# Two tiles of neighbour sums moved from TensorE matmuls to adding row gathers on GpSimd, passes 3 to 7

## The chip, the cores and the metric

One core of a Trainium2 chip runs the whole program in one launch. The metric is the device time of a launch in microseconds (us); lower is better. Times inside a launch come from one profiled execution.

## The reference, cut to what matters

Two point-cloud layers follow each other. Each of the two batches has 1024 points with 1024 coordinates (`ctx`) and 512 channels (`x`).

```
# layer 0
idx = top_k(-d2(ctx), 8)                   # 8 nearest points, per point
for i in range(4):
    p = leaky_relu(x, 0.01)
    c  = w_center[i] @ p
    gn = w_neighbor[i] @ p[:, idx]         # summed over the 8 neighbours
    x  = (c + gn.sum(neighbours)) / 9 + x
# layer 1
idx = top_k(-d2(ctx), 30)
att = softmax(small network of the neighbours' relative position)
x   = x + sum_k att[k] * x[:, idx[k]]
```

`w_center` and `w_neighbor` are the same input, two 512 x 512 matrices; block 0 uses the first and blocks 1 to 3 the second (an index past the end is clamped). So p and the sum over its neighbours can be added before one product.

## The kernel before, in words

In layer 0 the own point and its 8 neighbours enter with one weight, so the kernel sums the rows of p first and multiplies by the weights after. The sum is a matmul with a 0/1 matrix: `nbr[b]` is 1024 x 1024, has a one where column point takes row point as a neighbour, and a one on the diagonal for the point itself. All of this is done in two parts for accuracy: `p_h` is p rounded to fp32r, `p_l` the rest.

Layer 0 is eight *passes*, `it` = 0 to 7: block `it // 2` of batch `it % 2`. A pass has two stages on TensorE:

- The *aggregation*: 8 units `j` = 0 to 7, each one bank of PSUM. Units 0 to 3 are the four channel tiles of the first 512 points (first half), units 4 to 7 those of the last 512 (second half). A unit is 16 matmuls (8 tiles `m` of source points, `p_h` and `p_l`), in `aggregate` (L1472). ScalarE rounds the result into `q_h` (`q_high`, L718), VectorE writes the rest into `q_l` (`q_low`, L997). Units use banks 0 to 2 in turn, so unit g waits for `q_low` of unit g - 3.
- The *products*, `wp`: 8 tiles `m` of 128 points, 12 matmuls each (L1494 to L1496), in banks 3 to 5 in turn. VectorE adds a tile to `X` in `x_update` (L1003). Product g waits for `x_update` of g - 3.

The p of the next pass is made during the products, in the memory that the old p leaves: ScalarE writes two halves of the leaky ReLU (`p_halves`, L704 and L705), GpSimd joins them (`p_join`, L495), ScalarE rounds (`p_high`, L711), GpSimd subtracts (`p_low`, L500). `p_second`, where the join is, and `p_l` are the same memory, so `p_low` writes over the joined p. The first two units of an aggregation run side by side and wait for `p_low` tile by tile.

Each of the 16 steps of a pass (8 units, 8 products) is a *slot* g = 16 it + s. Every engine's program is written out by hand as a loop over slots, in strict order on each engine. In a slot an engine also does a piece of other work, `side(g)`: selection of neighbours (passes 0 to 2), table lookups of the neighbours' coordinates (slots 45 to 60: passes 2 and 3), the small network with its batch norms, in VectorE and ScalarE steps that wait for each other (passes 4 to 6, `network` and the list `NET`), the index columns (slot 108, pass 6) and the one-hots and spread matmuls of the attention (pass 7, from slot 115). On VectorE `side(g)` stands ahead of `q_low` or `x_update` of the same slot. On ScalarE `p_halves` and `p_high` stand ahead of `side(g)`.

The lookups are fed by broadcasts of index rows from DRAM, 480 KB each, issued by SP into a ring of `NB` = 7 buffers. Behind layer 0 comes `attend`, the attention's own matmuls (L1620 to L1635).

## Time and profile before

| | us |
|---|---|
| three runs | 719.92, 721.95, 722.13 (median 721.95) |
| the profiled execution | 719.64, span 717.9 |
| TensorE busy | 700.1 (98%) |
| VectorE busy | 580.2 (81%) |
| ScalarE busy | 348.1 (48%) |
| GpSimd busy | 250.2 (35%) |
| mean granted TensorE clock | 0.995 of full |

By the starts of the aggregation's and the products' first matmuls in the trace, pass 3 runs from 297.6 to 382.7, pass 4 from 382.7, pass 5 from 433.5, pass 6 from 485.2 and pass 7 from 538.4 to 604.8; the products begin at 348.9, 411.7, 462.5, 515.2 and 575.3. PE is TensorE's matmuls, PEld its weight loads, DVE is VectorE, ACT ScalarE, POOL GpSimd, SP the engine that only issues transfers. A row of a timeline begins with its start and its duration in us, and names in brackets how long the engine was idle before and who released it.

### The profile page before, as it was taken

Reading aid. Unit: us, or ns where it says so; the run is one execution under the profiler, and the core shown is the slowest. Engines: PE = TensorE matmul, PEld = TensorE weight load, DVE = VectorE, ACT = ScalarE, POOL = GpSimd, SP = SyncE. Lnnn points to the kernel's source line nnn. Section 1 sums busy time; section 2 is a strip of 40 time slices with the busy share of each in tenths; the row PEclk is TensorE's granted clock in tenths of the full one; section 3 lists DMA queues with packets and bytes.
Section 4 is the critical chain, followed back from the end, with each engine's and each line's share of the span. In section 5 each row is a group of like instructions: output and inputs, shape, how many; then the busy total and the mean of one; then the engine's idle time right before and its main releaser. Section 6 shows DMA issues by size and latency. Waiting matters only on the chain.

```text
span 717.9 us, 13047 instructions
## 1 busy us (share of the span) xinstructions
PE 700.1 (98%) x5458; PEld 584.5 (81%) x5458; DVE 580.2 (81%) x863; ACT 348.1 (48%) x529; POOL 250.2 (35%) x216
## 2 busy tenths in 40 slices
PE   6999999999999999999999999999998999999998
PEld 4799899778888887888888888877886887888887
DVE  4699999999699899766789798677677799678831
ACT  6456556448417137766892263383472344223210
POOL 2259757646608237400164083064172000000000
PEclk9999999999999999989999999999999999999999
DMA  9510301100000114554400000000000000100101
GB/s 351 178 3 1 117 1 48 41 29 1 1 1 0 62 41 135 190 166 168 167 31 1 1 0 1 0 1 1 0 1 0 2 1 2 42 35 30 46 31 58
DMA packets 21564, 35.66 MB, mean 50 GB/s; under 512 B 10113, under 2 KB 10369, under 8 KB 21505
## 3 DMA queue, kind: packets, MB, share of 16 engines
q1 hardware_dynamic: 20976, 33.78, 14.1%
q10 hardware_dynamic: 528, 1.05, 0.5%
q8 instruction: 43, 0.70, 0.4%
q14 instruction: 17, 0.13, 0.1%
HBM read 30.50 MB, written 4.33 MB: 49 GB/s over the span
## 4 chain that ended last, share of the span: by engine, by line
PE 77%; DVE 12%; POOL 5%; ACT 4%; issue 2%; DMA 1%; SPq 0%; POOLq 0%; ACTq 0%; DVEq 0%
PE bank L1472 25%; PE bank L1494 6%; PE bank L1496 6%; PE bank L1495 6%; PE bank L1519 5%; PE bank L1581 4%; PE bank L1620 4%; PE bank L1622 4%; PE bank L1383 4%; PE bank L1621 4%; PE bank L1385 4%; PE bank L1384 4%; DVE idx L970 2%; DVE vals L968 2%; POOL pts_l L500 1%
## 5 line engine op out<-in xcount | busy, mean ns | idle before, releaser
L1472 PE MATMUL bank<-nbr,pts_h 128*128 128x512 f32 x512 | 203.5, 397 | 4.0 <-DVE pts_l L997 3.9
L1472 PE MATMUL bank<-nbr,pts_l 128*128 128x512 f32 x512 | 200.8, 392 | 0.0
L495 POOL TENSOR_TENSOR p_second<-p_first,p_second 128x512 f32<-128x512 f32 x58 | 77.2, 1335 | 196.1 <-ACT p_second L705 196.1
L1472 PEld LDWEIGHTS bank<-nbr,pts_h 128*128 128x128 f32 x512 | 97.1, 190 | 26.3 <-DVE pts_l L997 4.5
L1472 PEld LDWEIGHTS bank<-nbr,pts_l 128*128 128x128 f32 x512 | 97.0, 190 | 19.9 <-issue 0.2
L718 ACT CAST pts_h<-bank 128x512 fp32r<-128x512 f32 x64 | 37.0, 588 | 155.4 <-PE bank L1472 155.2
L1494 PE MATMUL bank<-wT,pts_h 128*128 128x512 f32 x256 | 101.6, 397 | 0.0
L1496 PE MATMUL bank<-wT,pts_l 128*128 128x512 f32 x256 | 99.8, 390 | 0.0
L1495 PE MATMUL bank<-wT,pts_h 128*128 128x512 f32 x256 | 99.7, 389 | 0.0
L997 DVE TENSOR_TENSOR pts_l<-bank,pts_h 128x512 fp32r<-128x512 f32 x64 | 43.7, 685 | 48.3 <-ACT pts_h L718 47.9
L500 POOL TENSOR_TENSOR pts_l<-p_second,pts_h 128x512 fp32r<-128x512 f32 x58 | 79.1, 1370 | 2.0 <-ACT pts_h L711 2.0
L1383 PE MATMUL bank<-pts_h 128*128 128x512 f32 (+3 forms) x192 | 69.1, 360 | 7.9 <-DVE pts_l L930 7.5
L840 ACT CAST nbr<-bank 128x512 fp32r<-128x512 f32 x64 | 35.2, 590 | 77.9 <-PE bank L1581 77.9
L1384 PE MATMUL bank<-pts_l,pts_h 128*128 128x512 f32 (+3 forms) x192 | 66.4, 346 | 0.0
L1385 PE MATMUL bank<-pts_h,pts_l 128*128 128x512 f32 (+3 forms) x192 | 66.3, 345 | 0.0
L1496 PEld LDWEIGHTS bank<-wT,pts_l 128*128 128x128 f32 x256 | 48.0, 188 | 10.2
L1494 PEld LDWEIGHTS bank<-wT,pts_h 128*128 128x128 f32 x256 | 48.1, 188 | 9.4
L1495 PEld LDWEIGHTS bank<-wT,pts_h 128*128 128x128 f32 x256 | 48.1, 188 | 9.4
L711 ACT CAST pts_h<-p_second 128x512 fp32r<-128x512 f32 x58 | 35.7, 616 | 31.2 <-POOL p_second L495 31.2
L1620 PE MATMUL bank<-pts_h,nbr 128*128 128x512 f32 x120 | 48.7, 406 | 0.6 <-DVE pts_l L1282 0.6
L1003 DVE SCALAR_TENSOR_TENSOR X<-bank,X 128x512 f32<-128x512 f32 x64 | 43.5, 682 | 5.5 <-PE bank L1496 4.8
L1383 PEld LDWEIGHTS bank<-pts_h 128*128 128x128 f32 x192 | 36.8, 191 | 13.0 <-issue 7.2
(212 smaller groups left out, 1341.0 us busy)
## 6 DMA issues: line engine op xcount, KB each, us to landing
more<-a_rows SPq DMA_DIRECT2D x17, 480.0 KB, 4.7
scratch<-a_rows SPq DMA_DIRECT2D x15, 480.0 KB, 4.7
X<-in_ctx SPq DMA_DIRECT2D x12, 512.0 KB, 6.0
out_dram<-X SPq DMA_DIRECT2D x15, 256.0 KB, 2.0
more<-in_ctx SPq DMA_DIRECT2D x4, 512.0 KB, 5.5
X<-in_x SPq DMA_DIRECT2D x2, 1024.0 KB, 5.9
X<-in_x SPq DMA_DIRECT2D x1, 1536.0 KB, 6.8
w_raw<-in_fside_BxSxS SPq DMA_DIRECT2D x1, 1024.0 KB, 11.4
```

The lines of the kernel that those rows point to most:

```text
L495: pool.tensor_tensor(p, a, b, ALU.subtract).then_inc(s_p32, 1)
L500: pool.tensor_tensor(p_l[:, m, :], parts(n)[2], p_h[:, m, :].bitcast(F32), ALU.subtract).then_inc(s_p1, 1)
L997: dve.tensor_tensor(q_l[:, j, :], bank[g % 3][:], q_h[:, j, :].bitcast(F32), ALU.subtract).then_inc(s_ql, 1)
L1003: dve.scalar_tensor_tensor(dst, bank[3 + g % 3][:], 1.0 / (K0 + 1.0), dst, ALU.mult, ALU.add).then_inc(s_xu, 1)
L1383: pe.matmul(o, pts_h[:, k, rows], pts_h[:, k, cols], start=(k == 0), stop=False)
L1384: pe.matmul(o, pts_h[:, k, rows], pts_l[:, k, cols], start=False, stop=False)
L1385: return pe.matmul(o, pts_l[:, k, rows], pts_h[:, k, cols], start=False, stop=(k == KT - 1))
L1472: mm = pe.matmul(bank[u % 3][:], p[:, m, t * P:(t + 1) * P], nbr[b][:, m, hf * HALF:(hf + 1) * HALF], start=(m == 0 and part_ == 0), stop= ...
L1494: pe.matmul(bank[3 + g % 3][:], q_h[:, q, cols], wT[:, hi, t, :], start=(t == 0), stop=False)
L1495: pe.matmul(bank[3 + g % 3][:], q_h[:, q, cols], wT[:, 1 - hi, t, :], start=False, stop=False)
L1496: mm = pe.matmul(bank[3 + g % 3][:], q_l[:, q, cols], wT[:, hi, t, :], start=False, stop=(t == CT - 1))
L1620: pe.matmul(o, lhs[0], rhs[0], start=(r == 0), stop=False)
```

## The change

In passes 3 to 7, the last two tiles of points (m = 6 and 7) no longer get their sum from the aggregation. Units 4 to 7 become 256 columns wide. Instead:

- SP stores every tile of the joined p to DRAM (`p_rows`, 256 KB a tile), and copies tiles 6 and 7 also into a sum buffer in SBUF (the own point's row).
- At the start of the pass GpSimd issues 16 indirect transfers: for each of the two tiles, for each of the 8 neighbours, a gather of 128 rows of p from DRAM that is added to the sum buffer as it lands. A gather waits for the one before it on the same buffer. In passes 3 and 7 a tile has one sum buffer (a chain of 8); in passes 4 to 6 it has two (chains of 4), which GpSimd adds at the end.
- TensorE transposes each finished sum with four 128 x 128 transposes, ahead of the products of tiles 4 and 5; ScalarE and VectorE make `q_h` and `q_l` of it (`gathered_q_high`, `gathered_q_low`), for the products of tiles 6 and 7.
- `p_low` waits for the store, and on GpSimd it runs two tiles behind the join, not one. In passes 5 to 7, `p_low` of tiles 0, 2 and 4 is VectorE's.
- The ring of broadcasts has 6 buffers, not 7, and the buffer of the attention's index columns moves out of `idx`, which the gathers still read.

```diff
-        NB = 7
+        NB = 6
...
+        SUMS = {3: ((0,), (1,)), 4: ((0, 1), (2, 3)), 5: ((0, 1), (2, 3)), 6: ((0, 1), (2, 3)), 7: ((0,), (1,))}
+        sums = [more[:, 3 - i // 2, i % 2 * HALF:(i % 2 + 1) * HALF] for i in range(4)]
...
+        def by_vector(n):
+            return n // NT in LOW_PASSES and n % NT in (0, 2, 4)
+        LOW_PASSES = range(5, ITS)
...
+        def gathered_at(it, m):
+            return m + 2 - (NT - gathered(it))
# SP
+            def store_p(n):
+                it, m = n // NT, n % NT
+                sp.wait_ge(s_p32, n + 1)
+                sp.dma_start(p_d[it % B][m * P:(m + 1) * P, :], p_second[:, m, 0:HALF]).then_inc(s_pd[m], 16)
+                e = m - NT + gathered(it)
+                if e >= 0:
+                    if tiles_gathered(it):
+                        sp.wait_ge(s_gt, tiles_gathered(it))
+                    i, count = own_landed(it, e)
+                    sp.dma_start(sums[i], p_second[:, m, 0:HALF]).then_inc(s_own[i], 16)
# GpSimd
             def p_low(n):
...
+                if it >= G_FIRST:
+                    pool.wait_ge(s_pd[m], 16 * (it - G_FIRST + 1))
...
+            def gather(it, e, n):
+                T = it % B * NT + NT - gathered(it) + e
+                i, count = landed(it, e, n)
+                if n == 0:
+                    pool.wait_ge(s_own[i], 16 * own_landed(it, e)[1])
+                elif n < len(SUMS[it][e]):
+                    if joined(it, -1):
+                        pool.wait_ge(s_join, joined(it, -1))
+                else:
+                    pool.wait_ge(s_sum[i], 16 * (count - 1))
+                first = i != SUMS[it][e][0] and n < len(SUMS[it][e])
+                pool.indirect_dma_start(out=sums[i], out_offset=None, in_=p_d[it % B],
+                                        in_offset=bass.IndirectOffsetOnAxis(ap=idx[:, T, n:n + 1], axis=0),
+                                        compute_op=ALU.bypass if first else ALU.add).then_inc(s_sum[i], 16)
+
+            def gathers(it):
+                for m in range(NT):
+                    pool.wait_ge(s_pd[m], 16 * (it - G_FIRST + 1))
+                for n in range(K0):
+                    for e in range(gathered(it)):
+                        gather(it, e, n)
...
+                        pool.tensor_tensor(sums[of[0]], sums[of[0]], sums[of[1]], ALU.add).then_inc(s_join, 1)
...
             for it in range(ITS):
+                if it in SUMS:
+                    gathers(it)
...
-                        if n % (2 * CT):
-                            p_low(n - 1)
-                        if n % (2 * CT) == 2 * CT - 1:
-                            p_low(n)
+                        behind = 2 if it + 1 >= G_FIRST else 1
+                        if n % NT >= behind and not by_vector(n - behind):
+                            p_low(n - behind)
+                        if n % NT == NT - 1:
+                            for k in range(n - behind + 1, n + 1):
+                                p_low(k)
# ScalarE, loop over m
+                    if 0 <= gathered_at(it, m) < gathered(it):
+                        gathered_q_high(it, gathered_at(it, m))
                     side(16 * it + NT + m)
# VectorE, loop over m
                     side(16 * it + NT + m)
+                    if 0 <= gathered_at(it, m) < gathered(it):
+                        gathered_q_low(it, gathered_at(it, m))
+                    if m >= 2 and it + 1 < ITS and by_vector(NT * (it + 1) + m - 2):
+                        p_low(NT * (it + 1) + m - 2)
                     x_update(NT * it + m)
# TensorE
+                w = HALF - hf * gathered(it) * P
...
-                            mm = pe.matmul(bank[u % 3][:], p[:, m, t * P:(t + 1) * P],
-                                           nbr[b][:, m, hf * HALF:(hf + 1) * HALF],
+                            mm = pe.matmul(bank[u % 3][:, 0:w], p[:, m, t * P:(t + 1) * P],
+                                           nbr[b][:, m, hf * HALF:hf * HALF + w],
...
+                if m >= NT - gathered(it):
+                    pe.wait_ge(s_gql, tiles_gathered(it) + m - NT + gathered(it) + 1)
...
+                    if 0 <= gathered_at(it, m) < gathered(it):
+                        turn_gathered(it, gathered_at(it, m))
                     wp(NT * it + m)
```

How the programs of the engines move is seen at three places. The first is GpSimd, from the end of pass 3 (the last joins and low parts of pass 4's p) to the joins of pass 5's p. Before:

```order
L495 TENSOR_TENSOR p_second<-p_first,p_second 128x512
L500 TENSOR_TENSOR pts_l<-p_second,pts_h 128x512 x2
L495 TENSOR_TENSOR p_second<-p_first,p_second 128x512 x2
L500 TENSOR_TENSOR pts_l<-p_second,pts_h 128x512
L495 TENSOR_TENSOR p_second<-p_first,p_second 128x512
```

And now, with `more` the memory of the sum buffers:

```order
L569 TENSOR_TENSOR p_second<-p_first,p_second 128x512
L580 TENSOR_TENSOR pts_l<-p_second,pts_h 128x512 x3
L637 DMA more<-p_rows,idx 128x512 x16
L653 TENSOR_TENSOR more<-more 128x512 x2
L569 TENSOR_TENSOR p_second<-p_first,p_second 128x512 x4
L580 TENSOR_TENSOR pts_l<-p_second,pts_h 128x512
```

Sixteen gathers and two adds stand between the last low part of one pass and the first join of the next.

The second place is VectorE in the products of pass 6, from the network's last step over the index columns (slot 108, beside the product of tile 4) to the attention's first work in pass 7. Before:

```order
L1038 TENSOR_TENSOR scratch<-scratch,small 128x16x30
L1233 TENSOR_SCALAR scratch<-idx 128x512
L1234 CAST scratch<-scratch 128x512
L1235 TENSOR_SCALAR scratch<-idx 128x512
L1236 TENSOR_SCALAR scratch<-scratch 128x512
L1003 SCALAR_TENSOR_TENSOR X<-bank,X 128x512 x4
L1247 CAST more<-att_h 128x128x2
```

And now:

```order
L1375 TENSOR_SCALAR scratch<-scratch 128x512
L1127 TENSOR_TENSOR pts_l<-bank,pts_h 128x4x128
L1136 TENSOR_TENSOR pts_l<-p_second,pts_h 128x512
L1142 SCALAR_TENSOR_TENSOR X<-bank,X 128x512
L1127 TENSOR_TENSOR pts_l<-bank,pts_h 128x4x128
L1142 SCALAR_TENSOR_TENSOR X<-bank,X 128x512
L1136 TENSOR_TENSOR pts_l<-p_second,pts_h 128x512
L1142 SCALAR_TENSOR_TENSOR X<-bank,X 128x512 x2
L1386 CAST more<-att_h 128x128x2
```

L1127 is `gathered_q_low`, L1136 VectorE's `p_low`, L1142 `x_update`: the low part of the gathered tile 6 stands behind the whole of slot 108's side work.

The third place is ScalarE beside it, slots 107 to 109. Now:

```order
L927 ACTIVATE scratch<-scratch 128x480
L818 ACTIVATE p_first<-X 128x512
L819 ACTIVATE p_second<-X 128x512
L825 CAST pts_h<-p_second 128x512
L838 CAST pts_h<-bank 128x4x128
L818 ACTIVATE p_first<-X 128x512
L819 ACTIVATE p_second<-X 128x512
L825 CAST pts_h<-p_second 128x512
L838 CAST pts_h<-bank 128x4x128
```

L927 is the network's exponential, L838 `gathered_q_high`, which stands behind `p_high` (L825) of the next pass, and so behind GpSimd's join of that tile.

## Rows read from the trace of the kernel before

**Rows 1.** The page: busy time, and the chain that ended last.
```profile
PE 700.1 (98%) x5458; PEld 584.5 (81%) x5458; DVE 580.2 (81%) x863; ACT 348.1 (48%) x529; POOL 250.2 (35%) x216
...
PE 77%; DVE 12%; POOL 5%; ACT 4%; issue 2%; DMA 1%; SPq 0%; POOLq 0%; ACTq 0%; DVEq 0%
```

**Rows 2.** Windows, L1472 alone, first half of pass 4's aggregation.
```profile
382.70:397.20 14.50, 14.50 (x65) 12.01 (x65) 1.00 0.00 0
```

**Rows 3.** Waits: us in total, times, longest; whole span, then 485 to 493.
```profile
PE bank L1472 <- DVE pts_l L997: 3.9, 3, 2.6
...
PEld bank L1472 <- POOL pts_l L500: 0.9, 2, 0.5
```

**Rows 4.** Windows, all engines: stretches of passes 3 to 7.
```profile
core 0: us, PE busy (x) PEld busy (x) DVE busy (x) ACT busy (x) POOL busy (x), PEclk, DMA share, GB/s
297.60:348.90 51.30, 50.84 (x855) 43.58 (x852) 31.88 (x65) 34.39 (x25) 1.86 (x2) 0.93 0.48 156
...
382.70:411.70 29.00, 29.00 (x130) 24.01 (x129) 24.75 (x27) 6.35 (x10) 2.73 (x2) 1.00 0.00 1
411.70:433.50 21.80, 21.80 (x98) 18.06 (x97) 20.87 (x24) 15.24 (x26) 17.13 (x14) 1.00 0.00 0
...
462.50:485.20 22.70, 22.18 (x99) 18.13 (x98) 17.68 (x37) 19.02 (x33) 13.99 (x11) 1.00 0.01 1
...
515.20:538.40 23.20, 23.20 (x111) 19.32 (x110) 19.29 (x42) 16.70 (x29) 16.68 (x15) 1.00 0.00 1
...
575.30:604.80 29.50, 29.50 (x329) 23.95 (x326) 29.50 (x39) 11.94 (x23) 0.00 (x0) 1.00 0.01 2
...
324.90:348.90 24.00, 24.00 (x428) 20.69 (x425) 15.60 (x33) 16.69 (x13) 0.00 (x0) 1.00 0.50 166
556.50:575.30 18.80, 18.80 (x199) 15.43 (x195) 13.32 (x17) 6.26 (x13) 0.00 (x0) 1.00 0.01 2
```

**Rows 5.** Timeline of TensorE at the end: 256 columns.
```profile
711.32 0.28 PE L1634 MATMUL bank<-pts_l,nbr 128*128 128x256 f32 x1
...
712.88 0.28 PE L1635 MATMUL bank<-pts_h,nbr 128*128 128x256 f32 x1
```

**Rows 6.** Timeline of TensorE: four transposes, then the aggregation of pass 7.
```profile
538.07 0.60 PE L1566 MATMUL bank<-ident,scratch 128*128 128x128 f32 x4
538.43 0.47 PE L1472 MATMUL bank<-nbr,pts_h 128*128 128x512 f32 x1
```

**Rows 7.** Transfers: issuing queue, count, KB each, median us to landing.
```profile
more<-a_rows SPq DMA_DIRECT2D x17, 480.0 KB, 4.7
...
X<-in_ctx SPq DMA_DIRECT2D x12, 512.0 KB, 6.0
out_dram<-X SPq DMA_DIRECT2D x15, 256.0 KB, 2.0
```

**Rows 8.** Timeline of VectorE in the products of pass 6.
```profile
534.06 1.88 DVE L1003 SCALAR_TENSOR_TENSOR X<-bank,X 128x512 f32<-128x512 f32 x3
```

**Rows 9.** GpSimd's instructions by form (mean ns), and one in its timeline.
```profile
L495 POOL TENSOR_TENSOR p_second<-p_first,p_second 128x512 f32<-128x512 f32 x58 | 77.2, 1335 | 196.1 <-ACT p_second L705 196.1
...
L441 POOL TENSOR_TENSOR scores<-scores,X 128x1024 f32<-128x1024 f32 x7 | 16.9, 2411 | 1.8 <-PE bank L1372 1.8
...
534.41 0.16 POOL L562 IOTA scratch<- 128x32 bf16 x1
```

**Rows 10.** Timeline of GpSimd and VectorE around pass 6.
```profile
479.22 1.65 DVE L1047 SCALAR_TENSOR_TENSOR scratch<-scratch 128x1440 f32<-128x1440 f32 x1
...
480.05 1.98 POOL L495 TENSOR_TENSOR p_second<-p_first,p_second 128x512 f32<-128x512 f32 x1 [3.63 <-ACT p_second L705]
...
489.52 2.54 POOL L500 TENSOR_TENSOR pts_l<-p_second,pts_h 128x512 fp32r<-128x512 f32 x2
...
517.91 2.55 POOL L495 TENSOR_TENSOR p_second<-p_first,p_second 128x512 f32<-128x512 f32 x2 [25.85 <-ACT p_second L705]
```

**Rows 11.** Timeline of ScalarE in the products of pass 5.
```profile
474.74 4.19 ACT L751 ACTIVATE scratch<-scratch,stat 128x480 f32<-128x480 f32 x6 [0.42 <-DVE stat L1099]
```

More of the change, by code:

```diff
@@ L110, in build @@
         more = sb("more", [P, 4, N], F32)
+        p_d = [nc.dram_tensor(f"p_rows{i}", [N, C], F32, kind="Internal").ap() for i in range(B)]
         a_rows = nc.dram_tensor("a_rows", [CHUNKS, P, P], BF16, kind="Internal").ap()
@@ L184, in parts, with gathered, tiles_gathered, landed @@
             return p_first[:, m, 0:HALF], p_second[:, m, 0:HALF], p_second[:, m, 0:HALF]
+        SUMS = {3: ((0,), (1,)), 4: ((0, 1), (2, 3)), 5: ((0, 1), (2, 3)), 6: ((0, 1), (2, 3)), 7: ((0,), (1,))}
+        G_FIRST = min(SUMS)
+        sums = [more[:, 3 - i // 2, i % 2 * HALF:(i % 2 + 1) * HALF] for i in range(4)]
+        def gathered(it):
+            return len(SUMS.get(it, ()))
+        def tiles_gathered(it):
+            return sum(gathered(i) for i in range(it))
+        def landed(it, e, n):
+            of = SUMS[it][e]
+            i = of[n % len(of)]
+            return i, sum(K0 // len(t) for q in SUMS if q < it for t in SUMS[q] if i in t) + n // len(of) + 1
+        def own_landed(it, e):
+            i = SUMS[it][e][0]
+            return i, sum(t[0] == i for q in SUMS if q <= it for t in SUMS[q])
+        def joined(it, e):
+            return sum(len(t) > 1 for q in SUMS if q < it for t in SUMS[q]) + sum(len(t) > 1 for t in SUMS[it][:e + 1])
+        def by_vector(n):
+            return n // NT in LOW_PASSES and n % NT in (0, 2, 4)
+        def lows_done(n):
+            return sum(by_vector(k) == by_vector(n) for k in range(n + 1))
+        LOW_PASSES = range(5, ITS)
         def slots(a, n=1):
@@ L231, in build @@
         s_p1 = sem("p_low_ready")
+        s_p1v = sem("p_low_by_vector_ready")
         s_wm = sem("wp_done")
@@ L235, in build @@
         s_m = sem("agg_done")
+        s_pd = [sem(f"p_rows_stored{i}") for i in range(NT)]
+        s_sum = [sem(f"rows_landed{i}") for i in range(4)]
+        s_own = [sem(f"own_rows_copied{i}") for i in range(4)]
+        s_join = sem("sums_joined")
+        s_gt = sem("gathered_q_turned")
+        s_gqh = sem("gathered_q_high_ready")
+        s_gql = sem("gathered_q_low_ready")
         s_xu = sem("x_updated")
@@ L381, in _ @@
                     u = 2 * CH * c + t
+                    for m in STORE_AT.get(u, ()):
+                        store_p(NT * G_FIRST + m)
                     if u == 0:
@@ L396, in _ @@
                                  .to_broadcast([P, KH * P])).then_inc(s_bc[u % NB], 16)
+            for n in range(NT * (G_FIRST + 1), NT * ITS):
+                store_p(n)
             for T in range(TILES):
@@ L544, in tables @@
                 pool.tensor_copy(tab_p[:, 2], tab_rest[:]).then_inc(s_tab, 1)
+            def gather(it, e, n):
[18 more added lines that the diff above has]
+                        gather(it, e, n)
+                for e in range(gathered(it)):
+                    of = SUMS[it][e]
+                    if len(of) > 1:
+                        for n in range(K0 - len(of), K0):
+                            i, count = landed(it, e, n)
+                            pool.wait_ge(s_sum[i], 16 * count)
+                        pool.tensor_tensor(sums[of[0]], sums[of[0]], sums[of[1]], ALU.add).then_inc(s_join, 1)
             for it in range(ITS):
+                if it in SUMS:
+                    gathers(it)
                 for s_ in range(16):
@@ L1498, in wp, with turn_gathered @@
                 mm.then_inc(s_wm, 1)
+            def turn_gathered(it, e):
+                of = SUMS[it][e]
+                if len(of) > 1:
+                    pe.wait_ge(s_join, joined(it, e))
+                else:
+                    i, count = landed(it, e, K0 - 1)
+                    pe.wait_ge(s_sum[i], 16 * count)
+                pe.wait_ge(s_ql, 2 * CT * (it + 1))
+                for t in range(CT):
+                    mm = pe.transpose(turned_bank(it, e)[:, t * P:(t + 1) * P], sums[of[0]][:, t * P:(t + 1) * P],
+                                      ident[:])
+                mm.then_inc(s_gt, 1)
             def turn_a(c):
```

39 lines of the change are left out of this document (33 added, 6 removed).

## The prediction

> **What bounds the kernel now.** I first read the busy lines and the chain that ended last: TensorE is busy 98% of the span and stands for 77% of the chain, VectorE for 12% [rows 1]. The page warns that TensorE's busy time is modelled, so I then looked at its pace inside a pass and at what it waits for. In a plain aggregation 65 matmuls of 512 columns fill a 14.50 us window [rows 2], one every 0.226 us, without a hole. What TensorE waited for on VectorE in all aggregations is 3.9 us [rows 3]. So passes 3 to 7 are bound by TensorE, and a column taken from it is worth its time, as long as the other engines keep up. The table of windows says how far they are from not keeping up: in pass 4 VectorE is busy 24.75 of 29.00 us in the aggregation and 20.87 of 21.80 in the products behind it; in pass 7 it is busy 29.50 of 29.50 us beside the products; in passes 5 and 6 17.68 of 22.70 and 19.29 of 23.20; GpSimd is nearly idle in the aggregations (2.73 of 29.00) and busy 17.13 of 21.80 behind them [rows 4].
>
> **The change, term by term.**
>
> *Narrower matmuls.* In each of five passes the second half of the aggregation (4 units of 16 matmuls) is 256 columns wide and not 512. The price of a 256-column matmul stands in the last product: 14 of them start between 711.32 and 712.88, 0.120 us apart [rows 5], although each has its own weight load. 64 x (0.226 - 0.120) = 6.8 us a pass, 34.0 us in all.
>
> *Transposes.* Eight a pass. A group of four started at 538.07 and the next matmul at 538.43 [rows 6]: 0.36 to 0.44 us for four, so 0.9 us a pass, 4.5 us in all. Were nothing else to bind, the sum would be 34.0 - 4.5 = 29.5 us.
>
> *Pass 3.* Here the aggregation alternates with the table lookups, each fed by 480 KB broadcasts that take 4.7 us [rows 7]; the DMA engines are 0.48 busy [rows 4]. A slot of the second half (4 in 24.00 us, [rows 4]) shortens from 6.0 to 4.3 us. ScalarE has 4.2 and VectorE 3.9 us of work in it (16.69 and 15.60 in the four), both a little less with narrower copies, so they just keep up. But the same broadcasts then come in three quarters of the time, and 256 KB gathers lie between them. I take 1.5 us off: pass 3 gives 6.8 - 0.9 - 1.5 = 4.4 us. One buffer less for broadcasts costs nothing, as six are still three slots of 4.3 us ahead of a 4.7 us landing.
>
> *Pass 7.* Its second half has spread matmuls and one-hots: 4.7 us a slot (4 in 18.80, [rows 4]), after the change 3.0; VectorE has 13.32 / 4 = 3.3 us in one, 0.3 less with the narrower low part, so it just keeps up. Behind it VectorE has no idle time and now makes two more low parts (0.6 us each, as three updates in a row took 1.88 [rows 8]). 6.8 - 0.9 - 1.0 = 4.9 us.
>
> *Gathers.* No row shows one. Two prices matter: G, how long GpSimd is held by one, and how long until it lands. For G the ends are GpSimd's shortest instruction, 0.16 us, and its longest common one, 2.41 us [rows 9]; I take 1.2 us, near its 128x512 work of 1335 ns, which goes through as many rows as a gather has. For the landing, 256 KB to DRAM took 2.0 us and 512 KB from DRAM 6.0 us [rows 7]; I take 2.7, nearer the transfer of the same size.
> In passes 4 to 6 GpSimd cannot start them before the last low part of p, which in pass 6 ended at 489.52 + 2.54 = 492.06 [rows 10], 6.9 us after the pass began at 485.2. Then come 16 G, a landing of 2.7 and the second add 1.3: the first joining of the next pass's p starts at J = start + 10.9 + 16 G, with 1.2 us at start + 30.1. The products start at + 22.2, and before, GpSimd's first joining came 2.7 us behind them (517.91 against 515.2); now it comes 7.9 behind.
> Who is queued behind that: ScalarE's copy p_high waits for the joining, the network's ScalarE steps and the gathered q_high stand behind p_high, and VectorE waits for these before its x_update and the gathered low part, which the product of tile 6 needs. In pass 6, the second joining ended at 520.46 and VectorE finished the index work, right behind which the gathered low part stands, at 534.06 [rows 8, 10]: 13.6 us. About 1.2 of it was slack, so it ends at J + 2.6 + 12.4 = J + 15, or start + 45.1; two products of 2.7 follow: 50.6 us where it was 53.2. Gain 2.6.
> In pass 5 the batch norm's six ScalarE steps (4.19 us [rows 11]) stand between: second joining J + 2.6, square root and coefficients 4.0, the six 4.2, two halves, two copies and the low part 3.0, then the two products 5.4: J + 19.2, 49.3 us, and about 0.7 for VectorE's own queue: 50.0 where it was 51.7. Gain 1.7.
> In pass 4 VectorE itself binds. Of its 29.00 - 24.75 = 4.2 us without work in the aggregation about half lies in the second half; it saves 4 x 0.3 on narrower low parts, and gets two gathered ones and three of p (5 x 0.6). So it finishes about when it did, and TensorE may run ahead of it by three banks only: the updates of tiles 6 and 7, some 2 us, may come after TensorE's end of the pass. I reckon 49.0 where it was 50.8. Gain 1.8. Moving three low parts from GpSimd costs VectorE 1.8 us a pass and buys GpSimd 3.9.
>
> *Stores and own copies.* 10 of 256 KB a pass, from SP, which has nothing else in passes 4 to 7. A low part now waits for its store, 2.0 us; two low parts stand between the last joining and the last low part, 2.6 us, so the store is covered and the second copy costs at most 1 us, inside the 6.3 us that TensorE takes to come to tile 7. TensorE waited 0.9 us there before [rows 3]. I put it at nothing; without the cover it is 1 us a pass. The first gather waits for the last store too, and the store is over before the last low part.
>
> *Sum.* 4.4 + 1.8 + 1.7 + 2.6 + 4.9 = 15.4 us. The profiled execution took 719.64 us (span 717.9); 719.6 - 15.4 = 704.2. The median of the runs shown is 2.3 us above it: **706 us**.
>
> **A rule against this.** GpSimd's joining at 480.05 took 1.98 us and not 1.3, beside a 1.65 us operation of VectorE with all its inputs in SBUF [rows 10]: the two engines hold each other up. So gathers in pass 4, where VectorE is fullest, may be held too. The Trainium skill (SBUF — State Buffer, "SBUF: two separate sides") goes further: while VectorE runs an operation in a two-port mode, GpSimd cannot write the descriptors of its own DMAs at all. By the row the sum stays as it is; by that rule every gather beside such an operation waits it out, which is the mechanism of the first rival below and its 734 us. For the landing the skill (DMA: Bandwidth & Descriptors, "Anatomy of one DMA") states about 2.0 us plus bytes over 436 GB/s, which makes an estimate of 2.6 us for 256 KB; the sum would be the same.
>
> **Rivals.**
> *GpSimd becomes the bound (0.18; slower).* Once GpSimd binds, passes 5 and 6 end at start + 30.8 and + 31.5 + 16 G by the sums above, and pass 4, where the fourth joining (J + 5.3), the copies and low parts (2.3) and two products (5.4) remain, at + 24 + 16 G. With a hold of 0.7 us, as in the row at 480.05, on every gather, G is 1.9 and they take 54.4, 61.2 and 61.9 where they took 50.8, 51.7 and 53.2, a loss of 21.8 against 9.3 gained in passes 3 and 7: 719.6 + 12.5 + 2.3 = 734 us. The sum is zero where 9.3 + 155.7 - 86.3 - 48 G = 0, G about 1.64. For it speaks the row of 1.98; against it, the mean of GpSimd's 58 joinings is 1335 ns [rows 9], so a hold is rare.
> *The full gain (0.22).* The next pass's work has enough room, the side work gives way and little but TensorE's columns count: passes 4 to 6 give 4.5 each, 4.4 + 13.5 + 4.9 = 22.8, and up to 29.5 if VectorE too gives way: 692 to 699 us. Needs G near 1.0 or below. Against it stands VectorE's full queue in pass 4, whatever G is.
> *The landing is long (0.10).* In passes 3 and 7 each tile's eight gathers are a chain of one sum. In pass 7 the first transposes stand some 31 + 15 = 46 us after its start; from 7 on, eight links fit if one (G and its landing) is below 4.9 us. With 1.2 + 2.7 it holds. With 5.5 a link, which is below the 6.0 of 512 KB, the chain ends at 51, 5 us late, and the four rounds of passes 4 to 6 take 22.0 for 19.2, 2.8 later in each: 706 + 13.4 = 719 us.
> *Partial gain as summed (0.50).* 700 to 716 us, from G of 1.0 to 1.45.
>
> **From cases to numbers.** Faster by over 0.3%, about what a measurement of this kernel can tell from no change, is below 719.8 us: all of the full gain and the partial gain, and a few hundredths of the long landing: 0.75. Within 0.3%: the rest of the long landing, 0.07. Slower: 0.18. The range goes from 693, where only the best end of the full gain is left out, to 723, above which lies most of the first rival. The partial gain alone has 700 to 716.
>
> **What would show it.** The transposes and matmuls: 64 matmuls a pass 0.12 us apart. GpSimd's gathers: 16 in a row of 1.0 to 1.4 us each in passes 4 to 6, and its first joining some 8 us behind the first product. TensorE's new waits: before the products of tiles 6 and 7, for VectorE's gathered low part, 2 to 5 us in each of passes 4 to 6; none on the transposes in passes 3 and 7. Pass lengths of 49.0, 50.0 and 50.6 us. I am wrong if a gather holds GpSimd over 1.6 us, if TensorE waits on the sums themselves, or if in passes 5 and 6 it does not wait at all.

## The result, and the profile after

The changed kernel takes **758.06 us** (median of 4 runs, 754.33 to 760.58), the kernel before 721.83 beside it: a ratio of 1.0512 [1.049, 1.0533]. Forecast were 706 us, 693 to 723. The profiled execution took 758.07. From the page of the changed kernel, busy time and the chain that ended last (before: [rows 1]):

```profile
PE 689.7 (91%) x5498; PEld 579.5 (77%) x5498; DVE 586.6 (78%) x882; ACT 349.3 (46%) x539; POOL 372.7 (49%) x293
...
PE 49%; POOL 18%; DMA 18%; issue 8%; DVE 4%; ACT 3%; SPq 0%; POOLq 0%; DVEq 0%
```

GpSimd and DMA, 6% of the chain before, are 36% now. The table of windows, one row a pass (3 to 7), gives busy time and granted clock; the second fence is the sum row of the same five passes of the kernel before:

```profile
core 0: us, PE busy (x) PEld busy (x) DVE busy (x) ACT busy (x) POOL busy (x), PEclk, DMA share, GB/s
296.70:391.20 94.50, 82.62 (x1410) 71.83 (x1407) 61.92 (x116) 64.39 (x61) 47.70 (x34) 0.91 0.72 196
391.20:449.80 58.60, 48.84 (x233) 40.52 (x232) 47.61 (x54) 21.50 (x37) 42.28 (x31) 0.94 0.56 105
449.80:513.80 64.00, 50.30 (x235) 41.79 (x234) 42.15 (x75) 28.47 (x51) 45.74 (x32) 0.89 0.56 112
513.80:576.50 62.70, 51.67 (x250) 42.68 (x248) 41.68 (x92) 24.93 (x45) 43.43 (x33) 0.92 0.55 109
576.50:643.20 66.70, 59.60 (x608) 50.02 (x606) 56.98 (x84) 22.83 (x46) 32.99 (x20) 0.97 0.46 72
sum 346.50, PE 293.02 PEld 246.83 DVE 250.34 ACT 162.11 POOL 212.15; mean PE 58.60 PEld 49.37 DVE 50.07 ACT 32.42 POOL 42.43
```

```profile
sum 307.20, PE 303.52 PEld 252.03 DVE 241.83 ACT 160.40 POOL 87.90; mean PE 60.70 PEld 50.41 DVE 48.37 ACT 32.08 POOL 17.58
```

The five passes are 346.5 us long for 307.2. TensorE works 293.0 for 303.5, but stands idle 53.5 for 3.7. GpSimd's busy time went from 87.9 to 212.2 us.

Where the idle time comes from is read in GpSimd's timeline of pass 6, which starts at 513.8 and whose first product starts at 537.7:

```profile
517.06 1.55 POOL L637 DMA_INDIRECT more<-p_rows,idx  x1
518.91 1.55 POOL L637 DMA_INDIRECT more<-p_rows,idx  x1 [0.30 <-issue]
520.77 1.00 POOL L637 DMA_INDIRECT more<-p_rows,idx  x1 [0.30 <-issue]
522.07 0.99 POOL L637 DMA_INDIRECT more<-p_rows,idx  x1 [0.30 <-issue]
...
544.08 1.55 POOL L637 DMA_INDIRECT more<-p_rows,idx  x1 [0.30 <-issue]
545.93 1.56 POOL L637 DMA_INDIRECT more<-p_rows,idx  x1 [0.30 <-issue]
550.23 1.26 POOL L653 TENSOR_TENSOR more<-more 128x512 f32<-128x512 f32 x1 [2.74 <-DMA more<-p_rows,idx]
552.19 1.29 POOL L653 TENSOR_TENSOR more<-more 128x512 f32<-128x512 f32 x1 [0.70 <-DMA more<-p_rows,idx]
553.45 2.52 POOL L569 TENSOR_TENSOR p_second<-p_first,p_second 128x512 f32<-128x512 f32 x2
```

A gather that adds holds GpSimd 1.55 us, the two that overwrite 1.00, each with a gap of 0.30 behind it. Sixteen take 517.06 to 547.49, 1.90 us apiece. Then GpSimd waits for the sums (4.6 us from the end of the gather at 544.08 to the add at 550.23), adds them, and makes its first join at 553.45: 39.6 us after the pass began, 15.8 behind the first product. TensorE's longest waits from 391 to 577 us, passes 4 to 6:

```profile
PE bank L1640 <- DVE pts_l L1127: 12.2, 3, 5.7
PE bank L1655 <- POOL more L653: 12.0, 3, 6.2
PE bank L1640 <- DVE X L1142: 7.8, 3, 3.7
```

The second row is the transposes waiting for the sums. The first and third are products that wait for VectorE's gathered low part and its updates, which stand behind ScalarE, which stands behind the late joins. In passes 4 and 5 there is a shorter way as well. VectorE's own low part of the next p (`p_low`, L1136), which the change moved there, stands ahead of an update and waited for the store of a joined p, first in pass 4, then in pass 5:

```profile
DVE pts_l L1136 <- DMA p_rows<-p_second: 8.1, 1, 8.1
...
DVE pts_l L1136 <- DMA p_rows<-p_second: 14.5, 1, 14.5
```

No run takes these low parts back to GpSimd beside the gathers, so what this way costs by itself stays open.

A second cost follows the waits. TensorE's timeline in pass 6, and two windows over the same places:

```profile
559.08 0.80 PE L1640 MATMUL bank<-wT,pts_h 128*128 128x512 f32 x1 [3.68 <-DVE X L1142]
559.67 0.63 PE L1641 MATMUL bank<-wT,pts_h 128*128 128x512 f32 x1
560.10 0.63 PE L1642 MATMUL bank<-wT,pts_l 128*128 128x512 f32 x1
...
562.40 0.39 PE L1642 MATMUL bank<-wT,pts_l 128*128 128x512 f32 x1
562.63 0.40 PE L1640 MATMUL bank<-wT,pts_h 128*128 128x512 f32 x1
...
567.37 0.77 PE L1640 MATMUL bank<-wT,pts_h 128*128 128x512 f32 x1 [3.88 <-DVE pts_l L1127]
```

```profile
559.08:561.80 2.72, 2.72 (x6) 2.15 (x7) 2.65 (x4) 2.24 (x4) 2.72 (x2) 0.50 0.20 75
562.17:563.30 1.13, 1.13 (x6) 0.75 (x4) 0.99 (x4) 1.13 (x3) 0.53 (x2) 1.00 0.08 27
567.40:572.00 4.60, 4.60 (x11) 3.63 (x12) 4.38 (x5) 0.62 (x1) 3.83 (x3) 0.50 0.15 57
```

After each of these two waits of some 4 us the granted clock is 0.50 (1.2 GHz) for 3 to 5 us, and a 512-column matmul takes 0.43 us and not 0.23. TensorE's busy time hides this.

### The profile page after: what moved, and what is told of

The parts are those of the page before. It is cut to its first block, busy times and chain, and to the rows that moved or that the text cites. A ratio compares the mean times of both kernels' runs of the same rounds, so it can differ in the third digit from the quotient of the medians.

```text
span 756.3 us, 13366 instructions
## 1 busy us (share of the span) xinstructions
PE 689.7 (91%) x5498; PEld 579.5 (77%) x5498; DVE 586.6 (78%) x882; ACT 349.3 (46%) x539; POOL 372.7 (49%) x293
## 4 chain that ended last, share of the span: by engine, by line
PE 49%; POOL 18%; DMA 18%; issue 8%; DVE 4%; ACT 3%; SPq 0%; POOLq 0%; DVEq 0%
DMA more<-p_rows,idx 15%; PE bank L1616 10%; POOL more L637 9%; PE bank L1781 4%; PE bank L1783 4%; PE bank L1526 4%; PE bank L1782 4%; POOL p_second L569 4%; PE bank L1528 4%; PE bank L1527 4%; PE bank L1640 4%; PE bank L1641 3%; PE bank L1642 3%; PE bank L1740 3%; POOL pts_l L580 2%
## 5 line engine op out<-in xcount | busy, mean ns | idle before, releaser
L1616 PE MATMUL bank<-nbr,pts_h 128*128 128x512 f32 (+1 forms) x512 | 179.9, 364 | 6.3 <-DVE pts_l L1121 3.5
L1616 PE MATMUL bank<-nbr,pts_l 128*128 128x512 f32 (+1 forms) x512 | 177.0, 358 | 0.0
L637 POOL DMA_INDIRECT more<-p_rows,idx x80 | 126.1, 1576 | 67.1 <-DMA more<-p_rows,idx 45.2
L1640 PE MATMUL bank<-wT,pts_h 128*128 128x512 f32 x256 | 109.2, 427 | 20.2 <-DVE pts_l L1127 12.2
L1616 PEld LDWEIGHTS bank<-nbr,pts_l 128*128 128x128 f32 x512 | 97.6, 191 | 13.9 <-issue 0.2
L1641 PE MATMUL bank<-wT,pts_h 128*128 128x512 f32 x256 | 105.3, 411 | 0.0
L1642 PE MATMUL bank<-wT,pts_l 128*128 128x512 f32 x256 | 104.4, 408 | 0.0
L833 ACT CAST pts_h<-bank 128x512 fp32r<-128x512 f32 (+1 forms) x64 | 32.7, 522 | 135.2 <-PE bank L1616 126.6
L1640 PEld LDWEIGHTS bank<-wT,pts_h 128*128 128x128 f32 x256 | 51.6, 201 | 32.7 <-issue 13.4
L580 POOL TENSOR_TENSOR pts_l<-p_second,pts_h 128x512 fp32r<-128x512 f32 x49 | 67.7, 1389 | 16.3 <-DMA more<-p_second 7.9
L825 ACT CAST pts_h<-p_second 128x512 fp32r<-128x512 f32 x58 | 35.6, 614 | 76.1 <-POOL p_second L569 76.1
L1527 PE MATMUL bank<-pts_l,pts_h 128*128 128x512 f32 (+3 forms) x192 | 66.4, 346 | 0.0
L1642 PEld LDWEIGHTS bank<-wT,pts_l 128*128 128x128 f32 x256 | 51.5, 201 | 11.9
L1641 PEld LDWEIGHTS bank<-wT,pts_h 128*128 128x128 f32 x256 | 51.9, 203 | 10.0
L1121 DVE TENSOR_TENSOR pts_l<-bank,pts_h 128x512 fp32r<-128x512 f32 (+1 forms) x64 | 38.5, 605 | 24.9 <-ACT pts_h L833 24.2
L1142 DVE SCALAR_TENSOR_TENSOR X<-bank,X 128x512 f32<-128x512 f32 x64 | 44.0, 687 | 11.9 <-PE bank L1642 11.4
```

Of the source, the lines that this page charges most:

```text
L580: pool.tensor_tensor(p_l[:, m, :], parts(n)[2], p_h[:, m, :].bitcast(F32), ALU.subtract).then_inc(s_p1, 1)
L637: pool.indirect_dma_start(out=sums[i], out_offset=None, in_=p_d[it % B], in_offset=bass.IndirectOffsetOnAxis(ap=idx[:, T, n:n + 1], axis=0 ...
L1142: dve.scalar_tensor_tensor(dst, bank[3 + g % 3][:], 1.0 / (K0 + 1.0), dst, ALU.mult, ALU.add).then_inc(s_xu, 1)
L1527: pe.matmul(o, pts_h[:, k, rows], pts_l[:, k, cols], start=False, stop=False)
L1616: mm = pe.matmul(bank[u % 3][:, 0:w], p[:, m, t * P:(t + 1) * P], nbr[b][:, m, hf * HALF:hf * HALF + w], start=(m == 0 and part_ == 0), st ...
L1640: pe.matmul(bank[3 + g % 3][:], q_h[:, q, cols], wT[:, hi, t, :], start=(t == 0), stop=False)
```

## The experiments

Lengths of a pass go from its first aggregation matmul to the next pass's (pass 7: to its last product), in the one profiled execution. Times are medians, each ratio is to the kernel before as run beside it.

| | us | ratio | 3 | 4 | 5 | 6 | 7 |
|---|---|---|---|---|---|---|---|
| before | 721.8 | | 85.1 | 50.8 | 51.7 | 53.2 | 66.4 |
| changed | 758.1 | 1.051 | 94.5 | 58.6 | 64.0 | 62.7 | 66.7 |
| no_gathers | 704.8 | 0.978 | 80.7 | 50.9 | 48.3 | 50.8 | 62.8 |
| half_gathers | 707.8 | 0.983 | 80.6 | 50.8 | 48.3 | 51.4 | 63.1 |
| three_quarters | 715.8 | 0.993 | 85.4 | 51.0 | 56.7 | 50.9 | 62.9 |
| rest_alone | 721.8 | 1.001 | 83.6 | 50.8 | 51.7 | 54.0 | 67.6 |
| copies_on_sp | 720.0 | 1.000 | 92.4 | 50.6 | 48.2 | 51.9 | 61.2 |
| adds_later | 749.4 | 1.040 | 100.1 | 55.0 | 60.1 | 58.8 | 66.4 |
| no_adding | 713.0 | 0.989 | 83.9 | 51.2 | 53.0 | 51.2 | 62.8 |
| held | 738.2 | 1.025 | 79.0 | 57.4 | 64.3 | 62.7 | 61.1 |
| relu_after | 715.9 | 0.996 | 84.9 | 49.4 | 50.2 | 49.8 | 65.6 |
| relu_before | 714.1 | 0.991 | 85.1 | 50.7 | 51.1 | 52.5 | 64.0 |
| one_tile | 715.9 | 0.994 | 83.0 | 51.6 | 50.6 | 49.9 | 64.7 |
| one_tile_early | 718.8 | 0.996 | 88.3 | 47.9 | 48.9 | 51.3 | 72.3 |
| early_4_5 | 711.1 | 0.988 | 82.6 | 48.9 | 49.7 | 51.2 | 63.2 |
| two_buffers | 711.1 | 0.986 | 85.9 | 49.2 | 49.3 | 51.3 | 65.0 |

**How many gathers: none, 8, 12.**

```diff
-                for n in range(K0):
+                for n in range(KG):   # KG = 0, 4, 6
                     for e in range(gathered(it)):
                         gather(it, e, n)
```

> The changed kernel without its gathers: the sum of tiles 6 and 7 is the own row alone, one sum buffer a tile in every pass, no adds of two buffers. Narrow matmuls, transposes, stores, own copies, order of low parts and ring of six stay. Theory A (what costs is the time for which the gathers hold GpSimd, 1.55 us and a gap of 0.30 each, 29.6 us a pass) and theory B (what costs is how late the sums land) both give the full gain of the narrow matmuls: 690 to 700 us, with every pass shorter than before. Theory C (the rest of the change costs: stores, own copies, six broadcast buffers, low parts two tiles behind) keeps it above 720 us.

> The changed kernel with 4 of the 8 neighbours gathered, so 8 gathers a pass and not 16; the other four are left out of the sum. Theory A: the first join in passes 4 to 6 comes 8 x 1.85 = 15 us earlier than the 39.6 us behind the start of pass 6, so some 25 us behind it, about where the products begin; passes 4 to 6 take 48 to 51 us each and not 58.6 to 64.0, and pass 3 is shorter by some 8 us: 710 to 720 us. Theory B (landing): chains of two links in place of four in passes 4 to 6 end earlier too, and the time falls as much; the place differs, since TensorE's transposes, not the joins, are then what comes early. Theory C: 745 us or more.

> The changed kernel with 6 of 8 neighbours gathered (12 gathers a pass; two neighbours are left out of the sum). With 8 gathers the time was 707.8 us and with 16 758.1. Theory A (GpSimd's time): a pass has room for about 8 gathers between its last low part and the first join, and each further one costs its 1.85 us in each of passes 4 to 6 and half a chain's round, 3.5 us, in pass 3: half of the loss, 725 to 738 us, with the first join of pass 6 some 32 us behind its start. Rival A2 (only the landing of the last gathers and the two adds matter, by a fixed amount once the chain has four rounds and not by gather): below 715 us.

Measured: 704.80 [0.9755, 0.9795], 707.75 [0.9799, 0.9853], 715.79 [0.9896, 0.9958]. The first came 4.8 us above my range, the other two 2.3 and 9.2 below theirs. Eight gathers a pass are nearly free, 16 cost 53 us. Twelve cost less than I expected: passes 4 and 6 have room for them, pass 5, with the batch norm's ScalarE chain, has not (56.7 for 48.3), and pass 3 took 85.4 for 80.7. From 12 to 16, passes 4 to 6 grow by 7.6, 7.3 and 11.8 us, about four pitches of 1.90, or more. So each pass has a threshold, and the slope begins behind it. The run without gathers also bounds the whole idea, with the other work in this order. Its row of pass 5 and its sum row, by the columns above:

```profile
429.90:478.20 48.30, 45.74 (x235) 38.50 (x235) 40.86 (x73) 27.86 (x51) 18.47 (x14) 1.00 0.14 53
...
sum 293.50, PE 279.65 PEld 238.35 DVE 247.41 ACT 160.51 POOL 79.63; mean PE 55.93 PEld 47.67 DVE 49.48 ACT 32.10 POOL 15.93
```

TensorE's busy time falls by 23.9 us, but its idle time grows from 3.7 to 13.9 us (6.2 us of waits for VectorE's gathered low part in passes 4 to 6): of 29.5 us of columns 13.7 arrive in these passes, with gathers that cost nothing.

**The rest of the change alone.**

```diff
-        SUMS = {3: ((0,), (1,)), 4: ((0, 1), (2, 3)), 5: ((0, 1), (2, 3)), 6: ((0, 1), (2, 3)), 7: ((0,), (1,))}
-        G_FIRST = min(SUMS)
+        SUMS = {}
+        G_FIRST = 3
```

> The rest of the change alone: stores of p to DRAM, low parts behind the stores and two tiles behind the join, three low parts on VectorE in passes 5 to 7, ring of six; full 512-column matmuls, no gathers, no own copies, no transposes of sums. It computes the same as before. Theories A and B: within 3 us of the kernel before, 720 to 724 us. Theory C: 735 us or more, with pass 3 longer by some 9 us.

721.75 us, 1.0008 [0.9995, 1.0021]: the stores, the ring of six and the order of the low parts cost nothing that the time shows, as long as nothing is late. Theory C falls.

**The same transfers from another queue.**

```diff
+                sp.dma_start(sums[i], p_d[it % B][n * P:(n + 1) * P, :]).then_inc(s_copy[i], 16)
```

> In passes 4 to 7 the gathers are replaced by plain copies of 128 rows of p from DRAM into the same sum buffers, same number, same bytes, same chains, issued by SP (they overwrite and don't add, and read a whole tile, so the sums are wrong by that). Pass 3 keeps its gathers. It keeps the landings and the traffic and takes the hold off GpSimd. Theory A: passes 4 to 6 fall to 48 to 51 us each, pass 3 stays at 94.5: 715 to 725 us. Theory B: passes 4 to 6 stay above 56 us: 745 us or more.

719.99 us, 0.9996 [0.998, 1.0013]. Passes 4 to 6 are 50.6, 48.2 and 51.9 us, as without gathers; pass 3, which keeps its gathers, is 92.4. It is GpSimd's part in the transfer that costs, not the traffic. A plain copy may land sooner than an adding gather, so this run alone does not clear the landing.

**GpSimd held by something else.** The kernel without gathers, with this in their place in passes 4 to 6:

```diff
+                    for n in range(120):
+                        if held[0]:
+                            pool.wait_ge(s_held, held[0])
+                        held[0] += 1
+                        pool.iota(sums[2].bitcast(BF16)[:, 0:P], pattern=[[1, P]], ...).then_inc(s_held, 1)
```

> The kernel without gathers (704.8 us), with GpSimd kept busy at their place in passes 4 to 6 by a row of 120 short iotas into a buffer that nobody reads, each waiting for the one before, some 30 to 36 us a pass; the neighbours of the two tiles are left out of their sums. No transfer, no landing, no traffic is added. Theory A: passes 4 to 6 get as long as with the gathers, 57 to 64 us each (51.1, 48.4 and 50.6 without), so 725 to 742 us, by how long the row holds GpSimd, with TensorE's granted clock falling behind its waits. If GpSimd's time is not the cause: 705 us.

738.15 us, 1.0248 [1.0224, 1.0272]. Its GpSimd timeline in pass 5, and its windows of passes 4 to 6:

```profile
441.02 36.74 POOL L654 IOTA more<- 128x128 bf16 x120
477.73 2.49 POOL L571 TENSOR_TENSOR p_second<-p_first,p_second 128x512 f32<-128x512 f32 x2
```

```profile
377.40:434.80 57.40, 48.09 (x234) 39.79 (x233) 46.98 (x54) 21.46 (x37) 43.68 (x132) 0.91 0.08 31
434.80:499.10 64.30, 49.94 (x236) 41.40 (x235) 42.19 (x73) 28.15 (x51) 47.78 (x135) 0.87 0.12 45
499.10:561.80 62.70, 51.33 (x248) 42.69 (x247) 42.48 (x93) 25.15 (x46) 45.37 (x135) 0.92 0.12 46
```

The row of iotas, 36.7 us in each of the three passes, is as long as the gathers, landing and adds of the changed kernel (517.06 to 553.45, 36.4). The passes are 57.4, 64.3 and 62.7 us long, where the changed kernel has 58.6, 64.0 and 62.7, with TensorE's busy time within 0.8 us and the granted clock within 0.03, and not one gather. In passes 4 to 6 GpSimd's time between the last low part and the first join is enough for their whole loss. Here nobody waits for a sum, so the 12.0 us of waits on the transposes in the changed kernel are only the form that the same lateness takes.

**The hold of one gather, and the adds.**

```diff
-                                        compute_op=ALU.bypass if first else ALU.add).then_inc(s_sum[i], 16)
+                                        compute_op=ALU.bypass).then_inc(s_sum[i], 16)
```

> The changed kernel with all 16 gathers a pass as plain overwriting ones, none adds (so only the last neighbour of each buffer is in the sum). The gathers that overwrite held GpSimd 1.00 us and the adding ones 1.55 us. Theory A: 12 or 14 gathers a pass are 0.55 us shorter each, 6.6 us a pass: passes 4 to 6 are each 5 to 7 us shorter, 735 to 745 us in all. If the 1.55 us are not of the adding but of the place in the pass: no change, 755 to 760 us. In pass 3 the chain of landings stays, and 2 to 4 us are won at most, if overwriting lands as late.

```diff
                         p_join(n)
+                        if s_ == NT + 1:
+                            add_sums(it)   # waits for the sums and adds the two buffers
```

> The changed kernel with GpSimd's last waits for the sums and its adds of two buffers moved behind the second join of the next pass's p; same sums. Theory A: the first join of passes 4 to 6 starts right behind the last gather, some 6 us earlier (547.5 for 553.45 in pass 6), and passes 4 to 6 are 3 to 6 us shorter each: 740 to 748 us; passes 3 and 7 stay. If the landing and the adds cost nothing by themselves: 755 us or more.

713.02 us, 0.9891 [0.9845, 0.9938], 22 us below my range, and 749.35, 1.0396 [1.0376, 1.0416], 1.4 above it. Gathers by line, changed kernel first, then the one that does not add (busy us, mean ns of one, idle before them):

```profile
L637 POOL DMA_INDIRECT more<-p_rows,idx x80 | 126.1, 1576 | 67.1 <-DMA more<-p_rows,idx 45.2 <-issue 21.5
```

```profile
L637 POOL DMA_INDIRECT more<-p_rows,idx x80 | 81.1, 1014 | 55.6 <-DMA more<-p_rows,idx 39.0 <-issue 16.2
```

Adding makes a gather hold GpSimd half as long again. Without it 16 gathers fit as well as 12 adding ones. Passes 4 to 6 are 7.4, 11.0 and 11.5 us shorter, where I had expected 5 to 7. The hold explains 14 x 0.6 = 8 us a pass (two of the 16 overwrite in the changed kernel too); in passes 5 and 6 more goes, and TensorE's waits, with the slow matmuls behind them, are what is left to go. Passes 3 and 7 are shorter too, by 10.6 and 3.9 us. Moving the landing and the adds behind two joins gives 3.6 to 3.9 us a pass. Pass 3, where the edit changes nothing, was 100.1 us in this execution and 94.5 in the other: pass 3 with 16 gathers is not known better than that.

**GpSimd relieved of the joins.** In both kernels:

```diff
+                if n >= 24:
+                    act.activation(p_second[:, m, 0:HALF], src, ACT.Relu).then_inc(s_p32, 1)
+                    return
```

> The changed kernel, all 16 adding gathers a pass, but from pass 3's p on GpSimd makes no joins: ScalarE writes p in one step. It is relu(x) without the branch of -0.01, so the values of p are other ones (ScalarE saves one of its two steps a tile too). Theory A (GpSimd's time binds): a pass costs GpSimd 29.6 us of gathers, some 4 of landing, 3.3 of adds and 6.5 to 10.4 of low parts, 44 to 47 us, and nothing that ScalarE waits for stands behind the gathers, so TensorE's own 47 to 50 us bind again: passes 4 to 6 take 48 to 53 us, 705 to 720 us in all with pass 3 shorter too. If the gathers hurt in another way (their traffic, late sums): 740 us or more.

> The kernel before with the same cut (p = relu(x) in one ScalarE step and no join on GpSimd, from pass 3's p on; the branch of -0.01 is left out): the bound for what the cut alone gives. TensorE bound these passes, so 716 to 721 us by every theory.

715.9 us, 0.9955 [0.9921, 0.9989], and 714.13, 0.9905 [0.9883, 0.9927]. With nothing of ScalarE's behind the gathers, all 16 adding gathers fit: 49.4, 50.2 and 49.8 us. In pass 3, where the gathers end no sooner than in the changed kernel, the time falls from 94.5 to 84.9. But beside the kernel with the same relief the change is still no gain. That kernel came out 2 us below my range, mostly in pass 7, which I had not expected.

**One gathered tile.**

```diff
+        SUMS = {3: ((0,),), 4: ((0, 1),), 5: ((0, 1),), 6: ((0, 1),), 7: ((0,),)}
```

> One tile of points (m = 7) gets its sum by gathers and not two: 8 gathers a pass, second-half matmuls of 384 columns, four transposes a pass, one own copy; everything of the reference is computed. Theory A: the gathers are hidden, as in the run with half the gathers; TensorE gains at most 64 x 0.053 - 0.45 = 2.9 us a pass, 14.7 in all, of which the run without gathers suggests half to be kept: 707 to 714 us. Theory B (a gather chain costs by its landing, so one chain costs as two do in passes 3 and 7): 720 us or more.

715.85 us, 0.994 [0.9913, 0.9968], 2 us above my range, though GpSimd is no bound any more: the last two products of pass 4 took 9.2 us for 5.5. VectorE's timeline there, and TensorE's wait:

```profile
424.99 1.16 DVE L1300 TENSOR_TENSOR bank<-bank,scratch 128x960 f32<-128x960 f32 x1
...
426.88 0.69 DVE L1127 TENSOR_TENSOR pts_l<-bank,pts_h 128x512 fp32r<-128x512 f32 x1
```

```profile
PE bank L1640 <- DVE pts_l L1127: 1.9, 1, 1.9
```

Behind this wait a matmul started every 0.43 us again, up to 431.43, and not every 0.23. The gathered low part stood behind a slot of side work. So the transposes went two products earlier, in all passes, and then only in passes 4 and 5:

```diff
-            return m + 2 - (NT - gathered(it))
+            return m + 4 - (NT - gathered(it))                             # one_tile_early
+            return m + (4 if it in (4, 5) else 2) - (NT - gathered(it))    # early_4_5
```

> The kernel with one gathered tile, its transposes two products earlier (before product 3, and not 5); everything of the reference is computed. In the run with them before product 5, TensorE waited 2 us for VectorE's gathered low part in passes 4 and 5, which stood behind the side work, and took 9.3 and 8.0 us for the last two products where it took 5.6 before. If that order is the cause, 3 us come back in each of passes 4 and 5: 709 to 713 us. If VectorE's queue binds these passes whatever stands first: 714 to 717 us.

> One gathered tile, its transposes before product 3 in passes 4 and 5 alone, before product 5 in passes 3, 6 and 7; everything of the reference is computed. If the early place won 3.5 us in pass 4 and 1.7 in pass 5, and lost 5 in pass 3 and 7.6 in pass 7 since TensorE waited there for a chain of eight that was not done, the sum is that of the better places: 715.9 - 5 = 710 to 711 us, a ratio of about 0.985. If the difference in passes 4 and 5 was chance: 715 to 719 us.

718.82 us, 0.9955 [0.9926, 0.9985], above both of my ranges: passes 4 and 5 fell to 47.9 and 48.9 us, but 3 and 7 grew. In pass 7 a chain of eight is not done that early, and TensorE waited

```profile
PE bank L1655 <- DMA more<-p_rows,idx: 6.1, 1, 6.1
```

In pass 3 no wait of TensorE's for the sum is in the trace, and why it grew to 88.3 us is not shown. With the early place only in passes 4 and 5: **711.06 us, 0.988 [0.9857, 0.9902]**, as added up. This version beats both kernels.

```diff
+        SUMS = {it: ((0, 1),) for it in range(3, 8)}
+            return m + (2 if it == 6 else 4) - (NT - gathered(it))
```

> One gathered tile with two sum buffers in all five passes (chains of four links, one add), transposes before product 3, in pass 6 before product 5; everything of the reference is computed. If the landing of a chain's links sets passes 3 and 7, they are ready some 4 x 4.5 = 18 us earlier, TensorE does not wait for them even before product 3, and pass 3 gets shorter than the 83.1 us with one buffer: 708 to 711 us. If VectorE's order sets them, the early place costs again and pass 3 stays above 85 us and pass 7 above 66: 715 us or more.

711.06 us, 0.9861 [0.9831, 0.989], at the upper end of my range, but not as the theory had it: TensorE waited for no sum, yet pass 3 was 85.9 us and not below 83. The two versions can't be told apart.

## Why the prediction was wrong

**The step that failed is "for G ... I take 1.2 us".** The unit that counts is the pitch, 1.90 us: 1.55 of hold, 0.30 of gap behind it, and now and then a longer one. My first join stood at start + 30.1; it came at start + 39.6. The rule 10.9 + 16 G gives 41.3 with 1.90, which is near, but partly by luck: the first gather of pass 6 started at + 3.3 and not + 6.9, and landing and adds took 6.0 us behind the last gather and not 4.0. The break-even at 1.64 is not tested by any run. I had drawn G from GpSimd's arithmetic on a tile, a row of another kind of work, when its bounds were 0.16 and 2.41; the chances should have been spread over those, and more than 0.18 of them lay above 1.64. "I am wrong if a gather holds GpSimd over 1.6 us": the hold alone is 1.55, so I had also left out the gap. By my own sums this one term turns 706 us into the first rival's 734. The rest of the error lies, by the lengths of the passes, in pass 3 (13.8 us), in passes 4 to 6 beyond the rival's sums (7.8) and in pass 7 (5.2). In passes 4 to 6 I had priced VectorE's three low parts of p by their work alone, 1.8 us, and not by what they wait for.

**The first rival happened**, with its G of 1.9: it gave 54.4, 61.2 and 61.9 us for passes 4 to 6, and they took 58.6, 64.0 and 62.7. Its reason was not the right one. It wanted VectorE to hold up every gather by 0.7 us; the 80 gathers took 126.1 us, where 74 of 1.55 and 6 of 1.00 make 120.7. All that anything added to them is 5.4 us, of which some stood beside VectorE's work, as this one in GpSimd's timeline and the row of VectorE's beside it:

```profile
539.39 2.54 POOL L637 DMA_INDIRECT more<-p_rows,idx  x1 [0.70 <-issue]
```

```profile
538.84 1.66 DVE L1248 SCALAR_TENSOR_TENSOR scratch<-scratch 128x1440 f32<-128x1440 f32 x1 [1.89 <-ACT scratch L872]
```

That gather started 1.11 us before VectorE's operation ended and lasted 1.43 us beyond it. Of the 13 gathers of over 1.7 us, 12 fit this sum, the rest of the VectorE operation that ran at their start and 1.43 us; in passes 4 to 6 it comes to 1.2 us. The Trainium skill's rule of the port lock (SBUF — State Buffer, "SBUF: two separate sides") therefore explains at most 5.4 us of hold, where the rival wanted 0.7 on each of 48 gathers, 34 us. The gaps beyond 0.30 us, 6.2 us in passes 4 to 6, speak no more for it: in the kernel that does not add, every gap of these passes is 0.30 or 0.31 us.

**The long landing happened too**, in pass 7 and partly in pass 3. GpSimd's timeline in pass 7 of the kernel with one tile, a chain of eight on one buffer:

```profile
537.95 1.55 POOL L637 DMA_INDIRECT more<-p_rows,idx  x1
543.28 1.55 POOL L637 DMA_INDIRECT more<-p_rows,idx  x1 [3.78 <-DMA more<-p_rows,idx]
...
577.81 1.73 POOL L637 DMA_INDIRECT more<-p_rows,idx  x1 [3.82 <-DMA more<-p_rows,idx]
```

A link is (577.81 - 537.95) / 7 = 5.7 us, of which 4.1 are landing; I had taken 3.9 in all, and priced 5.5 as a rival. In pass 7 of the changed kernel the transposes waited 3.7 us ("none on the transposes in passes 3 and 7" was wrong), and the pass took 66.7 us for 62.8 without gathers. The Trainium skill says that the profile's interval of a GpSimd-issued transfer ends when its descriptors are made (Perfetto Trace Analysis, "DMA Instruction — SWDGE (GPSIMD)"); the rows agree, 1.55 us of hold and 4.1 more until the next may start.

**Pass 3** I counted as 4.4 us of gain. Without gathers it is that (85.1 to 80.7). With them it lost 9.4, because GpSimd stands in the chain and the next joins stand behind it. GpSimd's timeline, the first product being at 347.6:

```profile
358.51 1.55 POOL L637 DMA_INDIRECT more<-p_rows,idx  x1 [2.38 <-DMA more<-p_rows,idx]
361.28 1.56 POOL L637 DMA_INDIRECT more<-p_rows,idx  x1 [1.22 <-DMA more<-p_rows,idx]
362.27 3.08 POOL L569 TENSOR_TENSOR p_second<-p_first,p_second 128x512 f32<-128x512 f32 x2
```

I had checked the chain of pass 7 against the transposes, and that of pass 3 against nothing, though I wrote down who is queued behind the gathers for passes 4 to 6. With the joins off GpSimd (relu_after) pass 3 took 84.9 us, so the joins behind the gathers are 9.6 of its 13.8 us over the run without gathers, in one execution each; the same relief gave pass 3 nothing in the kernel before (85.1).

**What held.** The narrow matmuls:

```profile
405.70:413.40 7.70, 7.70 (x66) 7.70 (x65) 7.59 (x7) 1.71 (x4) 5.68 (x5) 1.00 0.90 126
```

7.70 / 66 = 0.117 us for 0.120. Stores and ring at nothing: rest_alone. VectorE as the bound of pass 4, by kind: it has no gain even without gathers (50.9 for 50.8, where I had put 1.8). It is the order on VectorE more than the amount: with one tile and early transposes the pass took 47.9. "The full gain", 692 to 699 us, was not to be had with the work in this order: the bound is 704.8, and my sum of 15.4 us with gathers at 1.2 us had spent nearly all of it. So the range had no room on its lower side either.

**Not in the prediction at all** was the clock. Against the run without gathers TensorE's busy time is 293.0 for 279.7 us with the same work: 13.4 us, a third of what its added idle time (53.5 for 13.9) is.

**Sum of the loss** against the run without gathers, 53.3 us: 33.4 is what holding GpSimd in passes 4 to 6 costs (held), the rest, 19.9, lies in passes 3 and 7 (15.5 and 5.6 us longer than in held, by the table, in one execution each). How a round of two gathers in pass 3 divides is shown in part by GpSimd's timeline there in the kernel that does not add:

```profile
307.24 1.14 POOL L637 DMA_INDIRECT more<-p_rows,idx  x1 [0.17 <-issue]
...
348.18 0.96 POOL L637 DMA_INDIRECT more<-p_rows,idx  x1 [0.30 <-issue]
```

A round took (358.51 - 306.18) / 7 = 7.5 us in pass 3 of the changed kernel and 5.6 in pass 7; without adding it took (348.18 - 307.24) / 7 = 5.8 in pass 3 and 4.0 in pass 7. So adding costs 1.6 us a round in both passes, and pass 3 costs 1.9 more than pass 7 either way. That the broadcasts are the cause of the 1.9 is not shown by any run.
